# A fused four-layer kernel: the attention planner places its maxima units by a clock of work

## What is computed

```python
# layer 0: self-attention (256 keys) with a gate, then cross-attention on the context (1601 keys), then an MLP
x = x + gate_a * (softmax(q k^T * hd**-0.5) v) @ W_proj      # q, k, v from modulate(ln(x))
x = x + softmax(q_c k_c^T * scale) v_c @ W_cproj             # k_c, v_c from ln(context)
x = x + gate_m * gelu(modulate(ln(x)) @ W_mlp1) @ W_mlp2
# layer 1: an expert layer with one-headed attention on the context (not touched by the change)
# layer 2: cross-attention on ln(context), no MLP
# layer 3: as layer 0, but its context is not normalised
```

## Time and profile before

| | us |
|---|---|
| median of 3 runs (lowest, highest) | 5723.09 (5717.75, 5727.13) |
| profiled execution | 5719.91 |
| its span, first to last instruction | 5718.1 |
| PE busy | 4820.5 (84%) |
| DVE (VectorE) busy | 3989.6 (70%) |
| ACT (ScalarE) busy | 3680.6 (64%) |
| POOL (GpSimd) busy | 1669.9 (29%) |
| granted clock of TensorE, mean of full | 0.945 |

### The profile page before, as it was taken

The page is one execution under the profiler, slowest core; times in us unless marked ns, Lnnn a source line. Parts: engine busy times, 40 slices in busy tenths (PEclk is TensorE's granted clock), DMA queues, the critical chain, the costliest instruction groups (busy, mean ns, idle before and its releaser), DMA issues.

```text
span 5718.1 us, 123215 instructions
## 1 busy us (share of the span) xinstructions
PE 4820.5 (84%) x47956; PEld 2303.5 (40%) x47956; DVE 3989.6 (70%) x8517; ACT 3680.6 (64%) x5027; POOL 1669.9 (29%) x2691
## 2 busy tenths in 40 slices
PE   3688888888888688876888888888888998888887
PEld 1233333333343267762333333343434443344333
DVE  3487777787777344445888787887777777777774
ACT  1366776676766444432777777777777776667666
POOL 2424334334322100013232423233222323222221
PEclk9699999999999899996999999999999999999998
DMA  1221111112110111111122111121212121111110
GB/s 42 64 61 44 51 54 50 52 46 58 44 52 26 37 30 32 32 28 57 46 59 60 55 49 56 51 64 51 64 52 59 39 59 43 50 40 51 40 44 7
DMA packets 362975, 271.11 MB, mean 47 GB/s; under 512 B 47911, under 2 KB 325002, under 8 KB 362396
## 3 DMA queue, kind: packets, MB, share of 16 engines
q1 hardware_dynamic: 362396, 263.23, 16.2%
HBM read 86.96 MB, written 12.78 MB: 17 GB/s over the span
## 4 chain that ended last, share of the span: by engine, by line
PE 32%; DVE 8%; ACT 6%; POOL 4%; issue 4%; SPq 0%; DMA 0%; ACTq 0%; POOLq 0%
PE pb_obank L914 12%; PE pb_dbank L927 8%; DVE pb_c_maxs L599 6%; ACT pb_probs L668 4%; PE pb_aunit L890 4%; PE pb_aunit L961 2%; PE pb_aunit L968 2%; POOL pb_c_cin L789 1%; PE pb_aunit L1001 1%; PE pb_dbank L975 1%; DVE pb_z_maxs L599 1%; POOL pb_c_hg L852 1%; PE pb_aunit L995 1%; POOL pb_c_cs_y L785 1%; ACT pb_c_ksp L712 1%
## 5 line engine op out<-in xcount | busy, mean ns | idle before, releaser
L599 DVE TENSOR_REDUCE pb_c_maxs<-pb_dbank 128x1 f32<-128x512 f32 (+1 forms) x3584 | 2048.7, 626 | 659.3 <-PE pb_dbank L927 646.6
L668 ACT ACTIVATE pb_probs<-pb_aunit 128x1024 f32<-128x1024 f32 (+1 forms) x1792 | 1756.5, 1025 | 465.3 <-PE pb_aunit L890 370.2
L599 DVE TENSOR_REDUCE pa_c_maxs<-pa_dbank 128x1 f32<-128x512 f32 (+1 forms) x1792 | 1027.6, 626 | 392.7 <-PE pa_dbank L927 387.4
L668 ACT ACTIVATE pa_probs<-pa_aunit 128x1024 f32<-128x1024 f32 (+1 forms) x960 | 942.9, 1025 | 260.4 <-PE pa_aunit L890 188.0
L927 PE MATMUL pb_dbank<-pb_c_kst,pb_c_qst 62*128 62x512 bf16 (+1 forms) x4096 | 886.5, 346 | 139.7 <-DVE pb_c_maxs L599 75.5
L914 PE MATMUL pb_obank<-pb_probs,pb_c_vaug 128*9 128x256 f32 x13312 | 893.2, 383 | 6.5 <-ACT pb_probs L668 6.3
L890 PE MATMUL pb_aunit<-pb_c_qst,pb_c_kst 64*128 64x256 bf16 x6144 | 597.9, 274 | 53.2 <-ACT pb_probs L668 21.3
L927 PEld LDWEIGHTS pb_dbank<-pb_c_kst,pb_c_qst 62*128 62x128 bf16 x4096 | 249.0, 94 | 778.8 <-DVE pb_c_maxs L599 561.0
L927 PE MATMUL pa_dbank<-pa_c_kst,pa_c_qst 62*128 62x512 bf16 (+1 forms) x2048 | 447.6, 353 | 62.8 <-DVE pa_c_maxs L599 24.2
L914 PE MATMUL pa_obank<-pa_probs,pa_c_vaug 128*9 128x256 f32 x6656 | 461.8, 393 | 1.1 <-ACT pa_probs L668 1.0
L914 PEld LDWEIGHTS pb_obank<-pb_probs,pb_c_vaug 128*9 128x9 f32 x13312 | 276.6, 90 | 377.2 <-issue 184.4
(11 more groups left out here) (475 smaller groups left out, 6607.0 us busy)
## 6 DMA issues: line engine op xcount, KB each, us to landing
pb_c_kst<-pb_c_ksp SPq DMA_DIRECT2D x384, 200.1 KB
pa_c_kst<-pa_c_ksp SPq DMA_DIRECT2D x192, 200.1 KB
pb_c_cin<-in_ctx SPq DMA_DIRECT2D x32, 768.0 KB
pa_c_cin<-in_ctx SPq DMA_DIRECT2D x16, 768.0 KB
moe_cin<-in_ctx SPq DMA_DIRECT2D x16, 768.0 KB
pb_c_qst<-pb_c_qsp SPq DMA_DIRECT2D x384, 32.0 KB
pa_z_qst<-pa_z_qsp SPq DMA_DIRECT2D x192, 32.0 KB
pa_z_kst<-pa_z_ksp SPq DMA_DIRECT2D x192, 32.0 KB
```

Source lines behind the costliest of these rows:

```text
L599: dve.tensor_reduce(dst, dbank[N % RING_D][:, 0:cnt * width].rearrange("p (s c) -> p s c", s=cnt), AX.X, ALU.max).then_inc(d_free, 1)
L668: act.activation(probs[u % RING_P][0:rows].rearrange("p a i q -> p (a i q)"), src[0:rows, :], ACT.Exp, scale=HD ** -0.5).then_inc(a_free, 1)
```

## The change

The order in which units `M` are placed is changed, and nothing else: no instruction is added or taken away, and `S`, `T`, `V` and the preparation keep their positions. A function `work_clock` walks all other tokens of a body in order of position, and adds PE's work of each (table `PE_WORK`) less VectorE's work of it (table `DVE_WORK`), never going back. Only tokens that the two items of this body have are counted (`present`). `by_work` then takes each `M` at its old share of the body and puts it at the position at which the clock has reached that share of its total, right behind the mark last passed. `Rn`, `Rt` and `mr` keep their distance in position from the `M` that they follow, and so move with it. `stage_list` now makes a plan for each kind of body, by the names of the two items in it.

```diff
-def body_plan(streams):
+PE_WORK = {"S": 0.23, "T": 0.23, "V": 0.5, "xt": 0.35, "q": 0.45, "ctx": 0.9, "k": 1.5, "v": 1.4, "o": 0.5, "ot": 0.35, "proj": 0.5,
+           "x2t": 0.35, "h": 1.8, "fc2": 1.9}
+PE_WORK_SELF = {**PE_WORK, "k": 0.45, "v": 0.45}
+DVE_WORK = {"ln": 0.75, "ln2": 0.75, "cs": 1.0, "ca": 1.6, "o": 0.6, "gm": 1.2}
+
+def present(tok, spec):
+    if spec is None:
+        return False
+    if tok[0] in ("cs", "ca"):
+        return bool(spec.ctx_ln)
+    if tok[0] in ("ln2", "x2t", "h", "tanh", "gm", "fc2"):
+        return bool(spec.mlp)
+    return True
+
+def work_clock(marks, kinds):
+    now, at = 0.0, [(0.0, 0.0)]
+    for pos, (s, _, tok) in sorted(marks, key=lambda m: m[0]):
+        if present(tok, kinds[s.key]):
+            pe = (PE_WORK if s.has_ctx else PE_WORK_SELF).get(tok[0], 0.0)
+            now += pe - DVE_WORK.get(tok[0], 0.0)
+            at.append((pos, max(now, at[-1][1])))
+    return at
+
+def by_work(clock, placed):
+    total, j, out = clock[-1][1], 0, []
+    for n, (pos, it) in enumerate(placed):
+        while j + 1 < len(clock) and clock[j + 1][1] <= pos * total:
+            j += 1
+        out.append((clock[j][0] + 1e-6 * (n + 1), it))
+    return out
+
+def body_plan(streams, kinds):
...
+    clock = work_clock(marks, kinds)
+    for s in streams:
...
         placed = spread([(s, 0, m) for m in ms[cut:]] + [(s, 1, m) for m in ms[:cut]], 0.0, 1.0, ws[cut:] + ws[:cut])
+        placed = by_work(clock, placed)
         marks += placed
...
 def stage_list(streams):
-    plan = body_plan(streams)
+    plans = {}
...
     for b in range(first, last + 1):
-        for s, off, tok in plan:
+        kinds = {s.key: s.items[b + s.lead][0] if 0 <= b + s.lead < len(s.items) else None for s in streams}
+        kind = tuple(spec and spec.name for spec in kinds.values())
+        if kind not in plans:
+            plans[kind] = body_plan(streams, kinds)
+        for s, off, tok in plans[kind]:
```

More of the change, by code:

```diff
@@ L246, in body_plan @@
         marks += [(pos, item) for item in group]
-    for s in streams:
-        ms, ws = [], []
-        for p in range(PAIRS):
-            for u, segs in enumerate(s.units):
-                ms.append(("M", p, u))
-                ws.append(110 + sum(width for _, _, width, _ in segs))
-        total, acc, cut = sum(ws), 0, 0
-        while acc < M_LEAD * total:
-            acc += ws[cut]
-            cut += 1
-        placed = spread([(s, 0, m) for m in ms[cut:]] + [(s, 1, m) for m in ms[:cut]], 0.0, 1.0, ws[cut:] + ws[:cut])
-        marks += placed
-        for pos, (_, off, m) in placed:
-            if m[2] == len(s.units) - 1 and m[1] in (3, 7):
-                half = m[1] // 4
-                marks.append((pos + 0.001, (s, off, ("Rn", half))))
-                lag = 0.040 if s.has_ctx else 0.100 if half == 0 else 0.160
-                marks.append((pos + lag, (s, off, ("Rt", half))))
-                marks.append((pos + lag + 0.001, (s, off, ("mr", half))))
     for s in streams:
@@ L309, in body_plan @@
             at(0.450, -1, "st")
+    clock = work_clock(marks, kinds)
+    for s in streams:
+        ms, ws = [], []
+        for p in range(PAIRS):
+            for u, segs in enumerate(s.units):
+                ms.append(("M", p, u))
+                ws.append(110 + sum(width for _, _, width, _ in segs))
+        total, acc, cut = sum(ws), 0, 0
+        while acc < M_LEAD * total:
+            acc += ws[cut]
+            cut += 1
+        placed = spread([(s, 0, m) for m in ms[cut:]] + [(s, 1, m) for m in ms[:cut]], 0.0, 1.0, ws[cut:] + ws[:cut])
+        placed = by_work(clock, placed)
+        marks += placed
+        for pos, (_, off, m) in placed:
+            if m[2] == len(s.units) - 1 and m[1] in (3, 7):
+                half = m[1] // 4
+                marks.append((pos + 0.001, (s, off, ("Rn", half))))
+                lag = 0.040 if s.has_ctx else 0.100 if half == 0 else 0.160
+                marks.append((pos + lag, (s, off, ("Rt", half))))
+                marks.append((pos + lag + 0.001, (s, off, ("mr", half))))
     marks.sort(key=lambda m: m[0])
```

## The result

The changed kernel takes **5953.9 us** (median of 4 runs, 5948.9 to 5956.2), the kernel before 5723.1: ratio 1.0403, interval 1.0385 to 1.0421. The sign of the forecast was wrong, and the time lies outside the range. The profiled execution spans 5952.1 us, against 5718.1.

A forecast was written before the change was run, and what follows sets the result against it. No engine was full: VectorE bound the quiet part of a body, PE the busy part, where VectorE idled. 5719.9 - 128 - 36 - 31 + 19 + 9 = 5553 us, 5556 against the median; range 5430 to 5728.

The forecast's parts named there:

- Regular bodies: Bodies behind the openings: units moved by work, larger of PE's and VectorE's work summed over gaps, gain 128 us.
- Buffering: Ring of three banks between PE and VectorE: buffers one and a half units, so sums over one and two gaps averaged.
- The wait at `Rt`: Layer 0, PE waiting 3.36 us for GpSimd's `mhl`: 3.0 of it goes in 12 bodies, 36 us.
- The clock: PE's halved clock behind waits in layers 0 and 3: part of it goes with fewer waits, 31 us.
- The openings: Bodies before the first of `pb` and `pa`: units bunched at the start delay other work, adding 19 and 9 us.
- Slower: Units side by side stall PE: 68 more at 0.9 us, plus 28 for openings, no gain, 5809 us; chance 0.14.
- No change: ScalarE's exponentials and evictions behind `k` set the pace; gain equals the openings' 28 us, 5720 us; chance 0.06.

The follow-up runs named there:

- The pairs: Kernel before, every second unit of the cross stream moved straight behind the one ahead, in one half of the body per run: 6143.2 and 6152.3 us.
- even_lag: even_apart with the second `Rt` of the cross stream set 3.5 hundredths of a body later: 5631.7 us, 0.9843.
- less: guard with units moved the other way, to 1.4 x even - 0.4 x clocked position: 5991.1 us, 1.0468.
- apart: guard with at most one unit of both streams between two pieces of TensorE's work, at clocked positions: 5714.0 us, 0.9993.
- The four kernels: Kernel before (even, 5723.1 us), guard (clocked, 5949.0), even_apart (5658.6) and apart (5714.0); the last two keep units from standing side by side.
- guard: Changed kernel, but units stay at even positions where the clock of work has a total of zero: 5949.0 us, 1.0411.
- even_apart: apart with even instead of clocked positions in its list of units: 5658.6 us, 0.9887.
- best: even_lag with `k`'s first projection moved ahead of the two value products of its step: 5685.3 us, 0.9946.
- pairs_busy: Kernel before, every second unit of the cross stream in positions 0 to 0.5 moved straight behind the one ahead: 6143.2 us, 1.0735.
- nodve_apart: apart with nothing taken off the clock of work for VectorE's other work: 5951.8 us, 1.0408.
- behind: guard with each unit put behind, not ahead of, the piece at which its share of the clock is reached: 5929.1 us, 1.0376.
- apart_lag: apart with the second `Rt` of the cross stream set 3.5 hundredths of a body later: 5787.7 us, 1.0119.

## Why the prediction was wrong

**Regular bodies, -128 us: this is the step that failed.** It said: "For every gap from one unit to the next I take the larger of PE's and VectorE's work and add up." The larger of three was wanted. A step of the quiet part holds two scores, and ScalarE empties them from a ring of two banks in 2 x 1.026 = 2.05 us, while TensorE needs 0.44 + 0.99 = 1.43 us for its scores and values, and 0.22 for a unit. Two units bring VectorE to 2.56; taking one away saves until 2.05 is reached, not down to 1.65. The stretch that takes the unit in pays its 1.28. How the steps add up is argued from durations. Shown are the quiet part that stayed at 34.4 us with 1.87 us of new waits for `probs` in it, the 119 us more of such waits in all, and the loss that halves with shorter exponentials. The sum had a gain in every kind but layer 0 alone, 128 us in all, where the bodies lost 193: 3.5 us each in layer 0 with `z`, 3 to 5.5 in layer 2 alone, near 5 in layer 2 with `z`, about 12 in layer 3 with `z`, and none in most of layer 3 alone.

**Buffering.** This is the second part of the same step. It had waits for VectorE fall, and they rose by 97 us. The mean of the sums over one and over two gaps credited the ring of banks with half of a pair of gaps. The pairs show the opposite, 0.77 us lost for each in both halves of the body, though this price is that of the even order only.

**The wait at `Rt`, -36 us: right in place, half in worth.** It fell from 3.35 to 1.24 us a body in layer 0, and what stands there is now ScalarE, as the step feared. In layer 3, costed at nothing, it appeared: 2.1 to 2.7 us with `z`, 1.93 alone, where it was 0.2. All waits for `mhl` fell by 28. In `even_lag` such a wait was worth about half of its length when it went.

**The clock, -31 us: nothing.** The mean is 0.947 against 0.945. Layer 0 rose from 0.95 to 0.98 and layer 3 alone from 0.94 to 0.99, as hoped, but in layer 2 with `z` it fell from 1.00 to 0.98, and in the four bodies of layer 3 with `z` from 1.00, 1.00, 0.98 and 0.98 to 1.00, 0.96, 0.90 and 0.95. The Trainium skill's rule on psum-queue depth-cycling ("TensorE: Matmul & The Clock Gate"), that small idles of TensorE between groups make the clock swing, agrees with these dips, and with 0.93 to 0.94 in the runs with pairs; it agrees less well with `less`, at 0.932 with hardly more neighbours. The mirror case is `apart`, whose 0.961 is what brings it level. In sum, nothing of the 231 us between the two kernels is clock.

**The openings, +28 us: 41.** The first scores of `pb` come 66 us behind its first maxima (2708.46 to 2774.48), where I expected 60 to 65 and it was 45. That is 21 of the 27 us of this opening, and 5 more lie between the first scores and the first eviction of `proj`. The maxima themselves do not start later: from the first matmul of `pb` to them it is 54.3 us, and was 54.8. What grew is only TensorE's wait in front of them, 28.58 us for 3.58, because item 1's preparation, which filled this time, now stands behind the units.

```profile
2708.46 1.01 PE L971 MATMUL pb_dbank<-pb_c_kst,pb_c_qst 62*128 62x512 bf16 x3 [28.58 <-DMA pb_c_kst<-pb_c_ksp]
...
2774.48 0.39 PE L934 MATMUL pb_aunit<-pb_c_qst,pb_c_kst 64*128 64x256 bf16 x4
```

**The rivals.** "Slower" had the side and one mechanism, but its 68 neighbours at 0.9 were a quarter of the loss, and it set the gain to zero where the placing itself had a price. "No change" named the other half, ScalarE's exponentials and evictions behind `k`, at a chance of 0.06, as something that hides a gain; it can also turn it. Added up, 52 for neighbours, some 115 for ScalarE and 29 to 41 for the openings make about 200 of the 231. These parts come from different pairs of kernels, so the sum fits but is not proved. The four kernels even or clocked, with neighbours or apart, put 171 us down to neighbours and the clocked order together. So ScalarE's exponentials and the units side by side are both shown as causes, and how the loss is shared between them stays open. Of `apart`'s gain of 235 us over `guard`, 95 are TensorE's shorter busy time (4830.4 to 4735.8), which goes with the higher clock.

## What to carry to other kernels

When work is moved between stretches of a loop, price each stretch by the slowest of *all* engines with a ring between them, at its count after the move: here the thinned stretch gave almost nothing back once the next engine set its pace, while the stretch that was filled paid in full. Spread evenly and forbid side-by-side first: that was worth 1.1% here, and with a later `Rt` 1.6%, without any model of costs. And a run that repairs the time need not have repaired the cause, nor does a loss that stays the same need to be the same loss; compare waits, busy time and clock before believing either.

## What was not expected of the hardware

VectorE's product of two tiles for the MLP (L714, 128x1024) takes 1.22 us in the kernels before and after the change, in `apart`, `even_apart` and `even_lag`, but in `best` 2.55 us in the mean, and 2.4 to 2.9 in 26 of 32 bodies: there it starts 0.3 to 0.8 us into GpSimd's L867, which reads two tiles as well. The instructions and shapes are the same. The page "GPSIMD Engine Reference" of the Trainium skill ("Specifications" and "Key points") says that GpSimd shares its interfaces to the on-chip memory with VectorE, and names instructions of VectorE with two inputs there as a case of contention. The trace agrees.

The runs show more: the one that starts second is the one that gets longer. Where they don't meet, GpSimd's instruction takes 2.12 us and VectorE's 1.22.

| first | second starts after, us | first takes | second takes | both together | runs |
|---|---|---|---|---|---|
| GpSimd | 0.31 | 2.12 | 2.9 | 3.2 | `best` |
| GpSimd | 0.52 | 2.12 | 2.68 | 3.2 | `pairs_busy`, `nodve_apart`, `behind` |
| VectorE | 0.67 | 1.22 | 2.52 | 3.2 | before, `even_lag` and others |
| VectorE | 0.45 | 1.22 | 2.75 | 3.2 | `even_lag` |
| VectorE | 0.27 | 1.22 | 2.93 | 3.2 | `apart`, `behind` |

In either order and at every offset the pair takes 3.2 us, little less than the sum of the two alone, 3.34: they run nearly one after the other. (GpSimd's spans are rough, but VectorE's rows alone say it.) In `apart_lag` VectorE comes second in 11 of 32 bodies, with 2.3 us, and in `pairs_busy` in 26 with 2.7, so a little of what those two runs lost may be this. So a move of `k`'s projection by one step, which moves the evictions and GpSimd's work behind it, can double an instruction of VectorE through GpSimd. No run took this overlap alone away, so the 54 us of `best` are put down to it by the trace only.
